# Attention on 64x32 tiles of the array in place of 64x64 and 128x32, with row maxima turned on VectorE

## The reference, cut to what matters

```python
# six layers, windowed
q = (x @ Wq.T + bq); k = (keys @ Wk.T + bk); v = (keys @ Wv.T + bv)   # 16 heads of 8
scores = einsum('bqhd,bkhd->bhqk', q, k) / sqrt(8)
scores = where((delta >= 0) & (delta <= 125), scores, neg)
attn = softmax(scores, axis=-1)
o = einsum('bhqk,bkhd->bqhd', attn, v) @ Wo.T + bo
x = _ln(x + o);  x = _ln(x + gelu(x @ W1.T + b1) @ W2.T + b2)
# one layer, causal over 512 keys
scores = q k / sqrt(8) + log(gate + EPS);  attn = softmax(where(causal, scores, -inf))
```

## Time and profile before

| | |
|---|---|
| Median of 3 runs | 1103.07 us (1100.26 to 1104.6) |
| Span of the profiled execution | 1102.7 us; no separate time of that execution is given, the span is what the sums are made against |
| TensorE matmul | busy 994.2 us, 90% |
| TensorE weight load | busy 705.4 us, 64% |
| VectorE | busy 809.7 us, 73% |
| ScalarE | busy 763.1 us, 69% |
| GpSimd | busy 407.5 us, 37% |
| Matmul instructions | 20080 |

### The profile page before, as it was taken

One profiled execution on the slowest core, in us unless ns is written; L12 is line 12 of the kernel. 1 busy time (PEld: TensorE's weight loads), 2 busy tenths in 40 slices (PEclk: granted clock), 3 DMA queues, 4 the chain that ended last, 5 costly groups with the idle time before them and its releaser, 6 DMA issues.

```text
span 1102.7 us, 47422 instructions
## 1 busy us (share of the span) xinstructions
PE 994.2 (90%) x20080; PEld 705.4 (64%) x20080; DVE 809.7 (73%) x2451; ACT 763.1 (69%) x1418; POOL 407.5 (37%) x544
## 2 busy tenths in 40 slices
PE   1679999999999999999998999998987988899993
PEld 0356777777777777777775777666664544555772
DVE  6777887777778887777777775879798979872320
ACT  7457666767777667767773777767767868688741
POOL 8711433333344433333344213444646353401311
PEclk9769999999999999999998999999999989999997
DMA  5522211222225211332224123221112020401220
GB/s 160 116 62 61 61 42 42 78 70 61 62 62 105 56 43 41 64 89 62 61 62 103 27 38 61 60 46 29 35 28 60 3 61 4 117 26 37 68 77 10
DMA packets 72627, 64.80 MB, mean 59 GB/s; under 512 B 16226, under 2 KB 66914, under 8 KB 72418
## 3 DMA queue, kind: packets, MB, share of 16 engines
q1 hardware_dynamic: 72418, 61.78, 23.3%
HBM read 15.70 MB, written 1.05 MB: 15 GB/s over the span
## 4 chain that ended last, share of the span: by engine, by line
PE 72%; DVE 11%; ACT 5%; POOL 5%; issue 3%; SPq 1%; DMA 1%; POOLq 0%; DVEq 0%; ACTq 0%
PE b L775 11%; PE b L887 9%; PE b L878 8%; PE b L676 7%; PE b L756 5%; PE b L790 4%; PE b L959 4%; PE b L949 4%; PE b L709 4%; PE b L806 2%; PE b L846 2%; PE b L871 2%; DVE mx L1218 2%; ACT probs L1021 2%; PE b L862 2%
## 5 line engine op out<-in xcount | busy, mean ns | idle before, releaser
L1021 ACT ACTIVATE probs<-b 128x443 f32<-128x443 f32 (+2 forms) x736 | 354.0, 543 | 137.5 <-PE b L756 96.5
L1218 DVE TENSOR_REDUCE mx<-b 128x2 f32<-128x378 f32 (+1 forms) x768 | 353.0, 508 | 93.9 <-PE b L709 93.5
L676 PE MATMUL b<-band,identb 64*64 64x252 bf16 x2304 | 170.4, 286 | 18.4 <-DVE mx L1218 8.1
L775 PE MATMUL b<-probs,vals 128*32 128x189 f32 (+5 forms) x3968 | 182.8, 311 | 1.2 <-DVE mx L1218 0.3
L775 PEld LDWEIGHTS b<-probs,vals 128*32 128x32 f32 x3968 | 115.1, 110 | 47.2 <-issue 12.2
L1543 POOL TENSOR_SCALAR veps<-mv 128x4 f32<-128x4 f32 x48 | 11.0, 230 | 352.4 <-DVE mv L1324 352.4
L756 PE MATMUL b<-qpack,kpack 64*64 64x189 bf16 (+5 forms) x3968 | 137.0, 236 | 0.3 <-issue 0.3
L709 PE MATMUL b<-kpack,qpack 62*64 62x189 bf16 (+1 forms) x3072 | 122.0, 239 | 1.0 <-issue 1.0
L676 PEld LDWEIGHTS b<-band,identb 64*64 64x64 bf16 x2304 | 67.0, 105 | 83.6 <-issue 36.5
L887 PE MATMUL b<-w,hid 128*128 128x128 f32 x768 | 110.1, 287 | 0.0
L1215 DVE TENSOR_REDUCE mx<-b 128x1 f32<-128x512 f32 (+7 forms) x256 | 99.3, 444 | 14.1 <-PE b L724 13.7
(11 more groups left out here) (173 smaller groups left out, 1695.7 us busy)
## 6 DMA issues: line engine op xcount, KB each, us to landing
kpack<-kparts SPq DMA_DIRECT2D x168, 128.2 KB
qpack<-qparts SPq DMA_DIRECT2D x168, 128.0 KB, 3.4
qpack<-mrows SPq DMA_DIRECT2D x224, 4.0 KB
w<-in_w SPq DMA_DIRECT2D x12, 256.0 KB, 4.3
w<-in_wa SPq DMA_DIRECT2D x12, 256.0 KB, 3.3
w<-in_wb SPq DMA_DIRECT2D x12, 256.0 KB, 3.7
rowt<-in_rowt SPq DMA_DIRECT2D x6, 384.0 KB, 3.4
stream<-in_x SPq DMA_DIRECT2D x4, 256.0 KB, 4.0
```

The costliest lines, as they stand in the source:

```text
L676: pe.matmul(out, identb[rows, rows], rhs.unsqueeze(1).to_broadcast([64, 2, 2, EDGE]), start=True, stop=False, skip_group_check=True)
L775: mm = pe.matmul(bank("sum", u, group)[32 * j:32 * j + 32, q0:q0 + w - skip], vals[:, u % 2, at:at + 32], probs[:, n % SETS, j, col + skip ...
L1021: act.activation(probs[:, n % SETS, j, 0:width], bank("exp", u, v, b)[:, 0:width], ACT.Exp, scale=SCALE).then_inc(a_emptied, 1)
L1218: red = dve.tensor_reduce(out[:, 2 * tb:2 * tb + 2], read[:, 0:2 * width].rearrange("p (t k) -> p t k", k=width), AX.X, ALU.max)
```

## The change

All three products of attention move to tiles of 64 rows by 32 columns, of which eight run side by side: two row halves (`e`, or `g` in the weighted sum) by four column quarters (`j`, or a lane).

- Keys and queries go in steps of 32. A chunk has 32 keys and at most 157 queries. A couple is now eight heads, and there are two couples. A windowed unit has 17 chunks in 5 banks (four of 3x157 = 471 columns, one of 129+97+65+33+1 = 325) and 5 banks of maxima (one of 65+65+129+129 = 388 columns, four of 471); a causal unit has 9 banks of each. A mask takes two edges of 31 columns for each of three tiles (186), or a whole first or last bank in one product.
- One bank of exponents now holds 8 heads by 32 keys by a couple, so a set of `probs` (4 banks) holds all 16 heads, and `weighted` does both former groups at once, into two `sum` banks, with 64 rows of contraction. `vals` is laid out for 17 chunks and 4 lanes; what doesn't belong to a head is nulled by a 0/1 column (`max_row[:, 1:3]`).
- The maxima of a unit are turned once, on VectorE (`dve.transpose` of 128x64 in 32x32 blocks), then split in two bf16 parts there; the TensorE transposes and ScalarE copies are gone. Four DMAs for a unit in place of eight, each from 128 partitions by 64 bytes into one row of `qpack`. All scores of a unit wait for all its maxima.
- v and the causal phase are projected on four 128x32 tiles.
- The planner's costs, biases and slacks are new, so the order of all jobs is another.

```diff
-CHUNK_BANKS = [[(0, 0, 189), (1, 189, 189), (7, 378, 65)],
-               [(2, 0, 189), (3, 189, 189), (6, 378, 129)],
-               [(4, 0, 189), (5, 189, 189), (8, 378, 1)]]
+SPAN = WINDOW + STEP      # 157
+TRIPLE = 3
+FULL = [[(TRIPLE * b + n, SPAN) for n in range(TRIPLE)] for b in range(4)]
+LEFT = [(c, SEQ + 1 - STEP * c) for c in range(12, NCHUNKS)]
+CHUNK_BANKS = [side_by_side(b) for b in FULL + [LEFT]]
+FIRST = [(0, 65), (1, 65), (2, 129), (3, 129)]
+TILE_BANKS = [side_by_side(FIRST)] + [side_by_side([(t + 4, w) for t, w in b]) for b in FULL]
...
-TURN_WORTH = 15422
+TURN_WORTH = 35444
...
-            def quarters():
-
-                return ((0, 0), (1, 1), (0, 1), (1, 0))
+            def tiles():
+
+                return ((0, 0), (1, 1), (0, 2), (1, 3), (0, 1), (1, 0), (0, 3), (1, 2))
...
+            def edges(bank, e, j):
+                out = pattern(bank[columns_of(j), 0:1], [SPAN, TRIPLE], [SPAN - EDGE, 2], [1, EDGE])
+                rhs = pattern(band[rows_of(e), 0:1], [0, TRIPLE], [SPAN - EDGE, 2], [1, EDGE])
+                pe.matmul(out, one(e), rhs, start=True, stop=False, skip_group_check=True)
...
+                    for e, j in tiles():
+                        rows, slot = slice(64 * e, 64 * e + BODY), 2 * j + couple
+                        first = slot * SEQ + 1 + STEP * t
+                        mm = pe.matmul(banks[e][columns_of(j), col:col + w], qpack[rows, buf, first:first + STEP],
+                                       kpack[rows, buf, slot, k0:k0 + w], start=False, stop=True, skip_group_check=True)
...
-            def weighted(u, group, b):
+            def weighted(u, b):
...
-                    for j in range(LANES):
-                        at = (c * PAIRS + LANES * group + j) * BLOCK
-                        mm = pe.matmul(bank("sum", u, group)[32 * j:32 * j + 32, q0:q0 + w - skip], vals[:, u % 2, at:at + 32],
-                                       probs[:, n % SETS, j, col + skip:col + w], start=(c == 0), stop=True,
+                    for g, lane in tiles():
+                        at = (c * LANES + lane) * BLOCK
+                        mm = pe.matmul(bank("sum", u, g)[columns_of(lane), q0:q0 + w - skip],
+                                       vals[rows_of(g), u % 2, at:at + STEP],
+                                       probs[rows_of(g), n % SETS, lane, col + skip:col + w], start=(c == 0), stop=True,
...
-            def turn_parts(u, half):
-                out = bank("parts", u, half)[:, :].bitcast(BF16)
...
-            def copy_parts(u, half):
...
+            def parts(u):
+                dve.wait_ge(d_emptied, emptied("max", u, LANES - 1, tops_of(u) - 1))
+                dve.transpose(turned[:, :, :].rearrange("p e q -> p (e q)"), mx[:, :, :, :].rearrange("p e c t -> p (e c t)")
+                              ).then_inc(max_turned, 1)
...
+                dve.tensor_scalar(mrows[:, u % 2, 0, :, :], turned[:, :, :], -1.0, None, ALU.mult).then_inc(negated, 1)
...
+            def load_max(u):
+                sp.wait_ge(mrows_ready, u + 1)
                 for part in range(PARTS):
+                    for e in range(2):
+                        row = 64 * e + BODY + part
+                        sp.dma_start(qpack[row:row + 1, u % BUFS, 1:1 + SLOTS * SEQ], mrows[:, u % 2, part, e, :]
+                                     ).then_inc(max_loaded[u % 2], 16)
```

More of the change, by code:

```diff
@@ new lines @@
+LATE = {"cat": 289002, "chosen": -912781, "cout": 814555, "eadd": -837587, "egelu": -1334, "ehid": -3780035, "eout":
+        25649, "exp": 139638, "expert": 233413, "gate": -50201, "gated": -342445, "gates": 105948, "heads": 347538,
+        "k": -212379, "logits": 223598, "max": 7199, "maxrows": 275775, "mix": 636170, "mixed": -124587, "mixin":
+        1770072, "mixv": 2056362, "nadd": -779717, "nroot": -46387, "nscale": -149044, "nstats": -95226, "ocat":
+        -480556, "open": 924332, "out": -373801, "phase": -1477370, "q": 187239, "recip": 308335, "rexp": 154530,
+        "router": -198535, "rows": 1066536, "score": 118627, "scored": -98974, "split": 183650, "spread": -126967,
+        "square": 89446, "state": 154023, "store": 217449, "sum": -8110, "take": 18873, "tanh": 377148, "top":
+        -21913, "turn": 767052, "v": 73638, "weigh": 12901, "weight": 85215, "window": 185319}
@@ L319, in unit_jobs @@
         values = ("even", u)
-    for couple in range(PAIRS // 2):
-        half = couple // 2
+    for couple in range(2):
         for tb in range(tops_of(u)):
-            cost = (267, 299, 299, 299, 160)[tb] if c else 246 if tb == 0 else 292
-            add("pe", ("max", u, couple, tb), cost, [("pack", "q", u), ("pack", "k", u), ("masks",)],
-                takes=[("max", u, 2 * couple + e, tb) for e in range(2)], mode=QUARTER, line="max")
+            width = width_of(tiles_of(u)[tb])
+            add("pe", ("max", u, couple, tb), cost_of_maxima(u, tb), [("pack", "q", u), ("pack", "k", u), ("masks",)],
+                takes=[("max", u, 2 * couple + e, tb) for e in range(2)], mode=SMALL, line="max")
@@ L354, in unit_jobs @@
+    for group in range(2):
+        add("act", ("sum", u, group), 487, [("weigh", u, banks_of(u) - 1), ("turn", u - 1, 1) if u else None],
             frees=[("sum", u, group)], line="sum")
@@ L811, in project_v @@
                     return
-                for h in range(2):
-                    mm = pe.matmul(bank("last", u)[64 * h:64 * h + 64, 0:64], state[:, u % BATCH, SEQ:KEYS],
-                                   wv[:, weights_of(u), 64 * h:64 * h + 64], start=True, stop=True)
+                for j in range(QUADS):
+                    mm = pe.matmul(bank("last", u)[columns_of(j), 0:STEP], state[:, u % BATCH, SEQ:KEYS],
+                                   wv[:, weights_of(u), columns_of(j)], start=True, stop=True)
                 mm.then_inc(d_filled, 1)
```

485 lines of the change are left out of this document (226 added, 259 removed).

## The result

The changed kernel takes 1355.89 us (median of 4, 1355.49 to 1357.75) against 1103.84 us (1100.26 to 1106.56) for the kernel before on the same chip: 1.229 times as long, 95% interval 1.225 to 1.232. The forecast was 1013 us, in a range of 975 to 1070. It was wrong in sign and by 343 us.

A forecast was written before the change was run, and what follows sets the result against it. TensorE, 98% busy in the windowed stretch, was taken to bound the kernel there. Saving 3.8 us a unit over 22 units gave 84 us, start and causal units 6: 1102.7 to 1012.7, stated as 1013 us, range 975 to 1070.

The forecast's parts named there:

- the supply rival: TensorE's maxima and scores: 688 small products a unit, fed at 18 ns each, +2.3 us a unit, 1153 us; chance within 0.11.
- its two companions: Eight tiles: bf16 at half rate (1136 us), or a floor for each product (0.02); with instruction supply 0.11 together.
- The threshold of 14.7 ns: Maxima and scores: time per product, over 688 a unit, above which slow instruction supply makes the change a loss.
- The clock: TensorE in windowed units: columns priced at 2.4 GHz, the full granted clock, with no change allowed for.
- v at nothing: Projection of v: same work on four tiles for two, costed at nothing.
- The moved wait: Scores wait for all maxima of a unit, not half; hidden by other TensorE work, taken as nothing, 5 us either way.
- Array time with shape changes, VectorE and ScalarE: Windowed unit: TensorE 30.5 to 26.4 us, including 1.0 saved on shape changes; VectorE about 21.6, ScalarE 19.2 us.
- The rule of the Trainium skill: TensorE: some 60 cycles overhead per matmul, 17 us for maxima and scores, kernel over 1,200 us; set aside on the trace.
- Busy 97%: Windowed stretch: TensorE busy 97% instead of 98%, giving a period of 27.2 us a unit.
- The rival of banks and other engines: Sum banks and unit-wide waits drop TensorE to 94% (28.1 us a unit, 1033 us) or 90% (1059); 0.18 for 1040 and above.
- The prediction's last sign: Causal stretch: the forecast is wrong if it becomes longer, as it has nine banks for five.

The follow-up runs named there:

- the last experiment: Kernel of its own alternating bursts of 64 to 1024 small products with whole-array products; its five stages last 88.1, 83.5, 97.6, 104.6 and 145.2 us.
- the last joined kernel: Changed kernel with windowed, causal, v, phase and causal mask products joined and no wait for the maxima; 1042.42 us, 0.945 times the kernel before.
- the supply measurement: Kernel of its own issuing long runs of products without waits, at several tile shapes and widths; 27.3, 26.8 and 27.6 ns a product over whole stages.
- the tenth experiment: Changed kernel in another order of jobs, its planner given a supply term and weights searched anew; 1449.74 us, 1.319 times the kernel before.

## Why the prediction was wrong

**The step that failed** is the price and the chance of the supply rival: "nothing shows the queue failing or holding", 18 ns a product, 1153 us, 0.11 with its two companions. The mechanism was right; the rate in it was mis-sized. It was taken from 20 products in 0.36 us (264.94 to 265.30), and the runs show 27 to 28 ns. Twenty products that stood ready say how fast the array eats, not how fast it is fed. A sustained rate needs a stretch longer than the reserve. Over eight units the trace of before had 5,505 products in 248.31 us, 45 ns each. Its densest 8 us, from 74.69, hold some 290 products, 28 ns each. And once it showed the queue failing:

```profile
223.06 0.36 PE L756 MATMUL b<-qpack,kpack 64*64 64x188 bf16 x12
224.91 0.30 PE L676 MATMUL b<-band,identb 64*64 64x252 bf16 x4 [1.49 <-issue]
```

The stop comes after 153 products in the 4.3 us from 219.13, the size of burst that stops the last experiment too. The DMA engines were 95% busy in those 4.3 us, so this row alone would not have proved the supply, but it was the one to ask.

With 28 ns in place of 18 the rival's own sum is 688x0.028 = 19.3 us for 6.0, +13.3-4.1 = +9.2 us a unit, a period of 40.2; measured are 40.0. So near a hit is partly luck: the sum counts maxima and scores alone and no change of the clock. A unit of the changed kernel has 1,160 products in all (34,912 are 24 of these, 4 causal units of 1,536 and the rest), and in the forecast period of 27.2 us that is 23 ns a product, a rate the forecast demanded and never put beside a row. The threshold of 14.7 ns leaves out the other 472 in the same way: 31.0 us over 1,160 is 26.7 ns.

The average alone doesn't make the loss. At 28.2 ns, the pace of the lots after the first 223, 1,160 products are 32.7 us a unit, and 22 units of 32.7 for 27.2 would be 1134 us. That it became 40.0 is the second half: the reserve. The small products stand in bursts, as the 126 of v at 411.85 us, and what the whole-array work leaves unused isn't saved beyond about one to two lots. The kernel before with its products cut in two shows this in a whole kernel: 35 ns a product on the average, slower than the supply, and still 103 us of stops. How the loss of the changed kernel divides between average and bursts wasn't measured.

**The clock** was a term at nothing, without a reason: the forecast took 2.4 GHz after as before. Over the twelve units TensorE is busy 5.2 us a unit more than forecast, at a granted clock of 0.90. An estimate from those rows: a fifth of 40.0 us at half speed, with TensorE busy four fifths of it, is some 3 us a unit, or 70 us in 22 units. It comes and goes with the stops (0.972 over the kernel before, 0.885 in the change, 0.921 with the windowed products joined, 0.943 in the last joined kernel), so the first difference below holds both, and no run separates them.

The account, all by runs:

| step | us | difference |
|---|---|---|
| the change | 1355.9 | |
| windowed products joined | 1128.8 | -227 |
| causal products joined | 1106.7 | -22 |
| v, phase, causal masks joined | 1066.5 | -40 |
| no wait for the maxima | 1042.4 | -24 |
| forecast | 1013 | -29 |

**"v at nothing"** failed. Its columns are the same, but 32 products a unit [L806 in rows 4] became 128 in a burst, and it is most of the 4,736 products of the 40 us. Without a stop the block of v takes 1.43 us to the next job (411.85 to 413.28), where L806 took 1.19. I read "four tiles for two" and missed that the product's other side shrank too.

**The moved wait, "I take nothing, with 5 us either way"**, failed: 24 and 26 us in two pairs. The idle row at 428.82 is one such wait. The landing of the 8 KB DMAs in 64-byte pieces, which no row had, is 4.8 us in the median, and scores of the unit stand behind all of it where a half stood before. "Other work hides it" held only where the planner had some left.

**Array time with shape changes, VectorE and ScalarE** were right in sum: 26.4 us of TensorE a unit as forecast, in the kernel without supply and wait (it has fewer groups of products, each of the 4 ns, and so flatters the figure by some tenths). The rule of the Trainium skill (TensorEngine Tiling (Array Packing), Instruction Overhead), some 60 cycles for each matmul, was rightly put aside as a cost of the array: by the supply measurement 128 products of 32 columns pass in 1.22 us. But 60 cycles at 2.4 GHz are 25 ns, an estimate by that page's rule, the supply sustains 27 to 28, and the "over 1,200 us" worked out from the rule was nearer than my number. It was so by another mechanism.

**"Busy 97%"** is 93% in that kernel, and 28.4 us a unit for 27.2 is 1.2x22 = 26 of the last 29 us, if the rest of the kernel came out as forecast, which wasn't measured apart. The rival of banks and other engines had said 28.1 us at 94%, 1033 us. So without the supply it would have been the rival, not the forecast, that came true. The prediction's last sign came true as well: from the first product of the causal phase to the last of L889 (L862 before), the causal stretch is 289 us for 242, and still 283 with the windowed products joined. The remaining waits are of many kinds, the largest with VectorE's names in the masks of the maxima:

```profile
PE b L731 <- DVE vals L1260: 6.2, 3, 2.1
PE b L734 <- ACT probs L1041: 3.7, 4, 1.2
...
PEld b L731 <- DVE mx L1226: 20.2, 37, 1.5
```

Which of them come from the order alone wasn't tried. Joining can also have changed things besides the number of products: the order was made for the kernel with stalls, and no order was made for the joined ones. And what in the new order of the tenth experiment delays VectorE and GpSimd stays open.

## What to carry to other kernels

Before cutting work into smaller products, divide the time of the stretch by the number of all the products you will have in it, not only of those you change: here TensorE was fed 128 products, each with its weight load, per 3.4 to 4.0 us, and below 28 ns a product nothing of the array's speed arrives. Bursts above some 150 products stall even where the average is far slower (no burst of 128 did; of six of 256, five did, and the sixth just behind it), so spread them among long products, or make them wide. Count also what the stops do to the clock. A rate read from a few operations in a row is the rate of the consumer; the supplier's needs a stretch that outlasts its reserve. Look too at what a cut does to every operand: columns that stay the same in sum can still be four times as many instructions.

## What the runs showed of the hardware

- TensorE's instructions came in packets of 16 KB, 128 products with their weight loads, every 3.4 to 4.0 us under full demand: 27.3, 26.8 and 27.6 ns a product for 157, 32 and 189 columns, on eight and on four tiles.
- Passed before the first stop of a burst, with what arrives meanwhile: 223 products after the first pause, 151 to 263 within the stages of bursts.
- Eight 64x32 tiles in bf16 run side by side at one column a cycle: a bank of 32 products with 657 columns for each tile, 0.27 us at 2.4 GHz, takes 0.30 us; at a granted clock of 0.50 it took 0.53 us.
- The granted clock is lower where TensorE stalls often: 0.91 from 300 to 600 us of the changed kernel, at 80% busy, 0.99 in the windowed stretch of the last joined one, at 93%. With the same order and waits, joining the windowed products took it from 0.885 to 0.921 over the kernel.
